# Down projections of a feed-forward stage as three fp32r products of upper and lower parts, in eight places

## What is computed

```
x = x + tanh(g_ffn[0]) * ffn(layernorm(x))

g = xf @ gate_w.T * gate_s            # [2048, 256] x [256, 704]
u = xf @ up_w.T * up_s
hdn = silu(g) * u                     # [2048, 704]
out = hdn @ down_w.T * down_s         # [2048, 704] x [704, 256]
```

## Time and profile before

| | before |
|---|---|
| time, median of 3 runs | 1323.59 us (1321.86 to 1324.62) |
| the profiled execution: time, span | 1321.55 us, 1319.8 us |
| TensorE (PE) busy | 1245.9 us, 94% of the span |
| VectorE (DVE) busy | 1084.2 us, 82% |
| ScalarE (ACT) busy | 966.9 us, 73% |
| GpSimd (POOL) busy | 701.7 us, 53% |
| chain that ended last, by engine | PE 78%, DVE 10%, issue 4%, ACT 3% |
| mean granted clock of TensorE | 0.986 |

### The profile page before, as it was taken

The page is one execution under the profiler, slowest core; times in us unless marked ns, Lnnn a source line. Parts: engine busy times, 40 slices in busy tenths (PEclk is TensorE's granted clock), DMA queues, the critical chain, the costliest instruction groups (busy, mean ns, idle before and its releaser), DMA issues.

```text
span 1319.8 us, 28439 instructions
## 1 busy us (share of the span) xinstructions
PE 1245.9 (94%) x10516; PEld 1086.0 (82%) x10516; DVE 1084.2 (82%) x2196; ACT 966.9 (73%) x2157; POOL 701.7 (53%) x612
## 2 busy tenths in 40 slices
PE   1678999999999999999999999999999999998998
PEld 1578899999999999999999999987776555555998
DVE  8979879999989999989999898986634778876654
ACT  5799888789987889898789897755322366674775
POOL 5666655656656557556556554433100255664685
PEclk9879999999999999999999999999999999998999
DMA  4212232231122322223321111222664413126762
GB/s 149 82 60 81 97 92 73 79 87 52 58 84 66 96 77 47 71 76 74 91 72 35 33 39 28 74 73 71 109 117 99 104 41 74 46 85 187 265 230 80
DMA packets 117511, 114.00 MB, mean 86 GB/s; under 512 B 12411, under 2 KB 102491, under 8 KB 116768
## 3 DMA queue, kind: packets, MB, share of 16 engines
q1 hardware_dynamic: 115152, 106.11, 28.9%
q0 software_dynamic: 2048, 6.05, 1.3%
q10 hardware_dynamic: 176, 0.04, 0.0%
HBM read 80.20 MB, written 32.00 MB: 85 GB/s over the span
## 4 chain that ended last, share of the span: by engine, by line
PE 78%; DVE 10%; issue 4%; ACT 3%; POOL 2%; DMA 2%; SPq 0%; POOLq 0%; ACTq 0%; DVEq 0%
PE PC L599 8%; PE PO L581 7%; PE SS L565 7%; PE B L542 5%; PE PA L498 4%; PE PA L500 4%; PE B L1293 3%; PE B L1784 2%; PE PA L512 2%; PE PA L511 2%; PE PA L510 2%; PE PC L589 2%; PE PO L1277 2%; PE B L555 2%; PE SS L568 2%
## 5 line engine op out<-in xcount | busy, mean ns | idle before, releaser
L1093 POOL TENSOR_TENSOR RB<-YS,M 128x512 bf16<-128x512 f32 x128 | 162.9, 1273 | 305.6 <-DVE YS L928 305.6
L718 ACT ACTIVATE QT<-B,sm 128x256 f32<-128x256 f32 x256 | 132.0, 572 | 42.0 <-PE B L542 41.9
L498 PE MATMUL PA<-WH,XQ 128*128 128x256 f32 x512 | 140.7, 306 | 17.2 <-DVE WL L874 13.3
L1088 POOL TENSOR_TENSOR yy<-vv,half 128x14 f32<-128x14 f32 (+1 forms) x64 | 147.9, 2311 | 5.3
L565 PE MATMUL SS<-QT,KT 128*128 128x256 f32 x512 | 131.8, 380 | 0.7 <-DVE mx L878 0.7
L500 PE MATMUL PA<-WL,XQ 128*128 128x256 f32 x512 | 130.1, 286 | 0.0
L898 DVE TENSOR_TENSOR QN<-QN,yy 128x512 f32<-128x512 f32 x128 | 127.5, 996 | 0.5 <-POOL yy L1088 0.5
L741 ACT ACTIVATE PPP<-SS 128x512 f32<-128x512 f32 x128 | 77.8, 608 | 65.8 <-PE SS L568 65.8
L890 DVE TENSOR_REDUCE vv<-SQ 128x7 f32<-128x896 f32 (+1 forms) x128 | 120.8, 944 | 0.3 <-ACT SQ L764 0.3
L498 PEld LDWEIGHTS PA<-WH,XQ 128*128 128x128 f32 x512 | 98.9, 193 | 18.8 <-DVE WL L874 13.7
L542 PE MATMUL B<-identf,QN 128*128 128x128 f32 x768 | 105.6, 274 | 2.0 <-ACT LNT L673 2.0
(11 more groups left out here) (354 smaller groups left out, 4109.3 us busy)
## 6 DMA issues: line engine op xcount, KB each, us to landing
W<-in_w SPq DMA_DIRECT2D x16, 1024.0 KB
XK<-xk_d SPq DMA_DIRECT2D x24, 512.0 KB, 4.3
V<-v_d SPq DMA_DIRECT2D x112, 64.0 KB
v_d<-VST SPq DMA_DIRECT2D x48, 128.0 KB, 2.1
Q<-qsc SPq DMA_DIRECT2D x8, 768.0 KB, 10.6
WR<-in_wprojT SPq DMA_DIRECT2D x16, 256.0 KB, 3.0
xk_d<-XK SPq DMA_DIRECT2D x8, 512.0 KB, 3.9
kt_d<-KT SPq DMA_DIRECT2D x64, 64.0 KB, 1.7
```

What stands on the lines that cost most here:

```text
L498: pe.matmul(PA[:, 256 * k:256 * k + 256], XQ[:, k, c, bs], wh[:, c, 256 * k:256 * k + 256], start=c == 0, stop=False)
L718: a.activation(QT[i % 2][:, o:o + 256], B1[:, o:o + 256], ACT.Identity, bias=col(n + "b"), scale=col(n + "w"))
L1088: p.tensor_tensor(yy[j % 2][:, :, 0:n], v_, half[:, 0:2 * n].rearrange("p (h k) -> p h k", h=2), ALU.pow).then_inc(s_rstd, 1)
L1093: p.tensor_tensor(RB[i % 2][:], YS[:], M[:], ALU.subtract).then_inc(s_rb, 1)
```

## The change

Hidden features and down weights are split into an fp32r upper part and the fp32r lower remainder, and a down projection is three products of parts per slice: 18 matmuls where there were six. `dve_hidden` now writes back into `SG`; ScalarE copies the upper part to `HS` or `HS2` (`act_hidden_upper`), VectorE subtracts it for the lower part (`dve_hidden_low`, semaphore `s_hl`). `HS` and `HS2` are eight places that slices take by turns (`i % 8`). `SG` is free again when the lower part is done. The down weights are scaled in quad 0, their upper part is made by ScalarE, their lower part by GpSimd.

The downs of a quad now follow slice 1 of the next quad, for three quads; the last four stand in `pe_attention_1`. Raw blocks 0 to 3 move into quad 3, query transposes and projections move by some slices, keys parts move later by up to a slice or two, masks move to quad 2, and the mask row is loaded into another place. Quad 0's queries are loaded back only behind the masks.

```diff
@@ -1176,19 +1176,32 @@
...
-        HD = [sb(f"HD{i}", [128, NI, 512]) for i in range(2)]
...
+        HS = sb("HS", [128, NI, 2, 512], FR)
...
+        HS2 = sb("HS2", [128, 2, 2, 512], FR)
+        DW = DWS[:, 0:NI * H].rearrange("p (n c) -> p n c", n=NI)
+        DS = DWS[:, NI * H:NI * H + H]
...
@@ -1197,14 +1210,16 @@
...
+        def hidden_part(i, z):
+            slot = i % 8
+            return HS[:, slot, z, :] if slot < NI else HS2[:, slot - NI, z, :]
...
@@ -1218,7 +1233,7 @@
...
-            return {(0, 4): 0, (0, 5): 1, (1, 0): 2, (1, 1): 3}.get((q4, n))
+            return {(0, 5): (0,), (1, 0): (1,), (1, 1): (2, 3)}.get((q4, n), ())
...
@@ -1240,12 +1255,14 @@
...
+                if q4 == 2:
+                    sp.wait_ge(s_up, NI)
+                    sp.dma_start(mrow, maskrow.broadcast_to([128, NT])).then_inc(s_row, 16)
...
@@ -1282,16 +1299,17 @@
...
-                pe.wait_ge(s_dw, 1)
+                pe.wait_ge(s_pl, G + 1)
                 pe.wait_ge(s_xf, 8)
             if j == 0:
-                pe.wait_ge(s_hd, NI * q4 + NI)
+                pe.wait_ge(s_hl, NI * q4 + NI)
             if b >= 2:
                 pe.wait_ge(s_fx, b - 1)
             for n in range(NI):
                 m = 128 if n < 5 else 64
-                t = pe.matmul(ps_[:, 0:H], HD[q4 % 2][0:m, n, 128 * j:128 * j + 128], DW[0:m, n, :], start=n == 0,
-                              stop=n == NI - 1)
+                for k, (z, w) in enumerate(((0, DWH), (0, DWL), (1, DWH))):
+                    t = pe.matmul(ps_[:, 0:H], hidden_part(NI * q4 + n, z)[0:m, 128 * j:128 * j + 128], w[0:m, n, :],
+                                  start=n == 0 and k == 0, stop=n == NI - 1 and k == 2)
             t.then_inc(s_down, 1)
...
@@ -1340,13 +1359,15 @@
...
-                    if q4 > 1 and n == 3:
-                        pe_query_turn(pe, q4 - 2)
-                    if q4 > 1 and n == 5:
+                    if q4 > 1 and n == 0:
                         pe_query_proj(pe, q4 - 2)
-                if q4 in (1, 2):
-                    for b in range(4 * q4 - 4, 4 * q4):
-                        pe_down(pe, b)
+                    if q4 and n == 1:
+                        for b in range(4 * q4 - 4, 4 * q4):
+                            pe_down(pe, b)
+                    if q4 in (1, 2) and n == 5:
+                        pe_query_turn(pe, q4 - 1)
+                    if q4 == 3 and n >= 2:
+                        pe_raw(pe, n - 2)
...
@@ -1370,9 +1391,23 @@
...
-                a.wait_ge(s_hd, i - 1)
+                a.wait_ge(s_hl, i - 1)
...
+        def act_hidden_upper(a, i):
+            m = 128 if i % NI < 5 else 64
+            a.wait_ge(s_hd, i + 1)
+            if i == NI:
+                a.wait_ge(s_pl, G + 1)
+            if i >= 8:
+                a.wait_ge(s_down, 4 * ((i - 8) // NI) + 4)
+            a.activation(hidden_part(i, 0)[0:m], SG[i % 2][0:m, :], ACT.Copy).then_inc(s_hi, 1)
+
+        def act_down_weights(a):
+            a.wait_ge(s_dw, 1)
+            a.activation(DWH[:, 0:5, :], DW[:, 0:5, :], ACT.Copy)
+            a.activation(DWH[0:64, 5, :], DW[0:64, 5, :], ACT.Copy).then_inc(s_ph, 1)
...
@@ -1416,14 +1450,20 @@
...
-                    if keys_parts_at(q4, n) is not None:
-                        act_keys_parts(a, keys_parts_at(q4, n))
+                    if q4 or n:
+                        act_hidden_upper(a, NI * q4 + n - 1)
+                    if q4 == 3 and n == 5:
+                        act_hidden_upper(a, NI * q4 + n)
+                    if q4 == 0 and n == 3:
+                        act_down_weights(a)
+                    for k in keys_parts_at(q4, n):
+                        act_keys_parts(a, k)
                     if q4 == 0 and n == 5:
                         act_last_turn(a)
-                    if q4 > 1 and n == 3:
-                        act_query_turn(a, q4 - 2)
-                    if q4 > 1 and n == 5:
+                    if q4 > 1 and n == 0:
                         act_query_proj(a, q4 - 2)
+                    if q4 in (1, 2) and n == 5:
+                        act_query_turn(a, q4 - 1)
...
@@ -1441,11 +1481,14 @@
...
-            v.scalar_tensor_tensor(out=HD[q4 % 2][0:m, n, :], in0=bank[i % 2][1][0:m, :],
+            v.scalar_tensor_tensor(out=SG[i % 2][0:m, :], in0=bank[i % 2][1][0:m, :],
                                    scalar=sm[0:m, AT["up_s"] + n:AT["up_s"] + n + 1], in1=SG[i % 2][0:m, :], op0=ALU.mult,
                                    op1=ALU.mult).then_inc(s_hd, 1)
+
+        def dve_hidden_low(v, i):
+            m = 128 if i % NI < 5 else 64
+            v.wait_ge(s_hi, i + 1)
+            v.tensor_tensor(hidden_part(i, 1)[0:m], SG[i % 2][0:m, :], hidden_part(i, 0)[0:m], ALU.subtract).then_inc(s_hl, 1)
...
@@ -1519,28 +1562,34 @@
...
-                    if keys_parts_at(q4, n) is not None:
-                        dve_keys_parts(v, keys_parts_at(q4, n))
-                    if q4 == 1 and n == 3:
-                        dve_down_weights(v)
-                    if q4 == 1 and n == 4:
-                        dve_mask_row(v)
-                    if q4 == 1 and n == 5:
-                        dve_masks(v)
+                    if q4 or n:
+                        dve_hidden_low(v, NI * q4 + n - 1)
+                    for k in keys_parts_at(q4, n):
+                        dve_keys_parts(v, k)
                     if q4 == 0 and n == 0:
                         dve_layer_root(v, 3)
                     if q4 == 0 and n == 1:
                         dve_layer_scale(v, 1, 3)
+                    if q4 == 0 and n == 3:
+                        dve_down_weights(v)
+                    if q4 and n == 1:
+                        for b in range(4 * q4 - 4, 4 * q4):
+                            dve_down(v, b)
+                        dve_layer_root(v, q4 - 1)
                     if q4 == 1 and n == 2:
                         dve_routing_constants(v)
-                    if q4 > 1 and n == 1:
-                        dve_layer_scale(v, 2, q4 - 2)
-                    if q4 > 1 and n == 5:
+                    if q4 and n == 3:
+                        dve_layer_scale(v, 2, q4 - 1)
+                    if q4 == 2 and n == 2:
+                        dve_mask_row(v)
+                    if q4 == 2 and n == 4:
+                        dve_masks(v)
+                    if q4 > 1 and n == 0:
                         dve_query_proj(v, q4 - 2)
-                if q4 in (1, 2):
-                    for b in range(4 * q4 - 4, 4 * q4):
-                        dve_down(v, b)
-                    dve_layer_root(v, q4 - 1)
+                    if q4 == 3 and n == 5:
+                        dve_hidden_low(v, NI * q4 + n)
+                    if q4 == 3 and n >= 2:
+                        dve_maximum_1(v, n - 2)
...
@@ -1564,6 +1613,9 @@
...
+            p.wait_ge(s_ph, G + 1)
+            p.tensor_tensor(DWL[:, 0:5, :], DW[:, 0:5, :], DWH[:, 0:5, :], ALU.subtract)
+            p.tensor_tensor(DWL[0:64, 5, :], DW[0:64, 5, :], DWH[0:64, 5, :], ALU.subtract).then_inc(s_pl, 1)
...
@@ -1696,7 +1748,9 @@
...
-                sp.wait_ge(s_hd, 12 * q4 + 12)
+                sp.wait_ge(s_up, 12 * q4 + 12)
+                if q4 == 0:
+                    sp.wait_ge(s_mask, 1)
...
@@ -1863,14 +1915,13 @@
...
-            for i in range(8):
+            pe_query_turn(pe, 2)
+            for i in range(4, 8):
                 pe_down(pe, 8 + i)
                 pe_raw(pe, i)
                 if i == 4:
                     pe_max_turn(pe, 0)
                 if i == 5:
-                    pe_query_turn(pe, 2)
-                if i == 6:
                     pe_query_proj(pe, 2)
...
```

More of the change, by code:

```diff
@@ L230, in build @@
         s_c, s_ch, s_ctx = (sem(n) for n in ("c", "ch", "ctx"))
-        s_sc, s_sr, s_srv = (sem(n) for n in ("sc", "sr", "srv"))
+        s_sc, s_sr = sem("sc"), sem("sr")
         s_rsm = [sem("rsm0"), sem("rsm1")]
@@ L1178, in build @@
         T16 = sb("T16", [128, 4096])
-        DW = sb("DW", [128, NI, H])
-        DS = sb("DS", [128, H])
-        HD = [sb(f"HD{i}", [128, NI, 512]) for i in range(2)]
-        GR = HD[0][:].rearrange("p n t -> p (n t)")[:, 0:4 * INTER].rearrange("p (w c n) -> p w c n", w=2, c=2)
+        DWH = sb("DWH", [128, NI, H], FR)
+        caus = sb("caus", [128, 128])
+        mcol = sb("mcol", [128, NB], I32)
+        fill4 = sb("fill4", [128, 112])
+        with nc.sbuf_tensor("GR", [128, 2, 2, INTER], F32) as GR:
+            pass
+        HS = sb("HS", [128, NI, 2, 512], FR)
+        with nc.sbuf_tensor("mrow", [128, NT], I32) as mrow:
+            pass
+        mrow = mrow[:]
+        mrf = mrow.bitcast(F32)
         XH, XL = [], []
@@ L1189, in build @@
         GL = sb("GL", [128, 2, 2, INTER], FR)
-        fill3 = sb("fill3", [128, 256])
         SG = [sb(f"SG{i}", [128, 512]) for i in range(2)]
+        DWL = sb("DWL", [128, NI, H], FR)
+        fill3 = sb("fill3", [128, 352])
```

(26 more changed lines are left out.)

25 lines of the change are left out of this document (8 added, 17 removed).

## The result

The changed kernel takes 1328.5 us (median; 1325.55 to 1333.69), the kernel before beside it on the same chip 1322.22 us (1320.43 to 1325.51). The ratio is **1.0048, 95% interval 1.0034 to 1.0062: 6.3 us slower**. The ratios of this document leave out one execution, of 3096.6 us, of the kernel e13. The forecast was "no change", with 1324.5; the time lies at the upper end of the range.

What follows compares the result with a forecast made beforehand. TensorE was taken as the bound. Saving 12.5 us and 0.3, against stops of 1.6, 1.6, 4.4, 4.4 and 1.0, gave +0.2 us, plus 0.8 for clock: 1322.5 profiled, 1324.5 forecast, range 1318 to 1328.5.

Steps and rivals of the forecast that it cites:

- 16 downs: TensorE's down projections: 18 fp32r products at 0.120 us, 2.16 us a block instead of 2.94, 12.5 us less in all.
- old idle time: TensorE's existing wait for a hidden slice around the end of quad 0 goes: 0.3 us less.
- stop 1: Slice 4: TensorE waits 1.6 us for gate product 6, as ScalarE's down-weight copies stand ahead of activation 4.
- stop 2: Slices 3 to 5: GpSimd holds VectorE's lower parts; TensorE waits 1.6 us, then 4.4 us before the first down.
- stop 3: Behind the second down: the third waits 4.4 us for VectorE's addition, queued behind keys parts and lower parts.
- small waits later: Three small TensorE waits in quad 3 and before the last four downs: 1.0 us more in all.
- low clock behind 937: Idle gaps of stops 2 and 3 may halve TensorE's clock; counted as 0.8 us more.
- old dip: Half clock near 1049 us in the kernel before, costing 1.5 us; the faster rival said it need not recur.
- Half its price: A clock dip of 1.5 us after stops 2 and 3 taken as about even odds, so 0.8 us counted.
- faster rival: Lower parts of slices 3 and 5 slip past GpSimd and no dip follows: 1320.1 us, tail to 1311; chance 0.28.
- slower one: TensorE's clock stays low past 948 us, longer than 5 us: 3.75 us more, 1327.5 us; chance 0.23.
- Late queries: Quad 0's queries, loaded behind the masks, arrive late for the first raw block: 1330 us or more; chance 0.03.

Runs made afterwards that it cites:

- e13: e12 with the load of quad 2's queries put back at its place in the changed kernel; ratio 0.9965 to the kernel before.
- e9: Changed kernel plus 15 useless products on TensorE ahead of its wait for the lower part of slice 5; ratio 1.0056 to the kernel before.
- e1: Changed kernel with the 64-row sixth slice padded to 128 rows with zero weights in every down projection; ratio 1.0022 to the kernel before.
- e5: Changed kernel with each down's three 64-row products placed singly between 128-row ones, six height changes a block instead of two; ratio 1.0183 to the kernel before.
- e2: Kernel before with the last slice padded to 128 rows, still six f32 products a block; ratio 0.9967 to the kernel before.
- e6: Changed kernel with GpSimd's lower part of quad 3's inputs held until the lower part of slice 5 is done; ratio 1.0053 to the kernel before.
- e4: Changed kernel with keys part 3 one slice later, behind slice 2 of quad 1; ratio 1.0040 to the kernel before.
- e14: e12 with the four keys parts moved behind slices 6, 8, 10 and 11; ratio 0.9937 to the kernel before, median 1314.98 us.
- e3: Changed kernel with quad 2's queries loaded behind the maxima of block 2 instead of block 1; ratio 1.0053 to the kernel before.
- e12: Changed kernel: padded slice, later quad 2 queries, later keys part 3, GpSimd's quad 3 lower part behind slice 5, down-weight scaling a slice earlier; ratio 0.9949 to before.
- e15: The changed kernel run once more, unedited; ratio 1.0046 to the kernel before, runs from 1324.64 to 1335.91 us.
- e10: Changed kernel with the four downs behind the third slice of the next quad instead of the second; ratio 1.0045 to the kernel before.

## Why the prediction was wrong

Right in kind: small against its parts, TensorE's saving given back in stops. Wrong in size by 5.5 us: the sum of the steps was +1.0 us, the traces show +6.6. By its own steps (the terms of the right column add up to +6.5):

| step | predicted | measured |
|---|---|---|
| 16 downs | -12.5 | -6.8 at full clock |
| old idle time | -0.3 | -0.3 |
| stop 1, gate 6 | +1.6 | +1.3 |
| stop 2, gate 7 and first down | +1.6, +4.4 | +0.8, +3.9 |
| stop 3, third down | +4.4 | +2.6, and 4.1 where the clock ahead is full (e9) |
| small waits later | +1.0 | +0.2 |
| low clock behind 937 | +0.8 | +1.6, taken off stop 3 |
| maxima row, its clock, old dip | 0 | +2.2 |
| rest of TensorE's work up to the first scores | 0 | +1.0 |

**What TensorE saves** is the step that failed: "nothing is cheaper than 0.120 there, and 0.13 (a switch between forms) would make it 9.6". The 0.120 was right for the product; the rows it came from have one height, and a down has two. (No row that the prediction names shows the 0.13 either.) e1 and e5 put the missing price at 0.19 us for each change of height. It stood in the trace of before: the 11.73 us of the earlier trace rows contain it as well (10.36 in e2), and the average of 0.244 a pass, 11.73 / 48, hid it. I divided a total by its count. TensorE's timeline of before puts the twelve passes of a block into one row and hides it too, but the timeline of its weight loads (PEld) shows two steps out of line, one on either side of the 64 rows:

```profile
945.41 0.29 PEld L1293 LDWEIGHTS B<-DW,HD 64*128 64x128 f32 x2 [0.33 <-issue]
946.03 0.94 PEld L1293 LDWEIGHTS B<-DW,HD 128*128 128x128 f32 x5 [0.33 <-issue]
```

The loads of this line sat idle for 8.7 us in 28 such places in the kernel before, and for 1.4 us in 6 once padded (e2).

The step is worth 5.7 us, as much as the whole error; 16 x 0.32 = 5.1 of it are the changes of height. The other errors cancel almost: the stops are 8.8 us and not 13.0, while the low clock costs 0.8 more than forecast, and the maxima row (2.2) and the rest of TensorE's work (1.0) were put at nothing.

**The stops** were found at the right instructions and with the right releasers, and the forecast made each somewhat too long; at gate product 7 that is because lower part 3 ended behind the first of GpSimd's two subtractions and not behind both. e6 confirms the hold by GpSimd (0.67 without, 1.62 with), and e4 and e14 the keys ahead of the additions. The prediction extended the hold to the lower parts from the Trainium skill's GPSIMD Engine Reference (1. Specifications), which says that GpSimd shares its SBUF interfaces with VectorE instructions of two SBUF inputs. The trace agrees: 2.20 and 1.62 us beside GpSimd, 0.67 alone.

**"Half its price" for a clock dip** was the wrong question. The dip came (0.61 and 0.82 in the windows of 3 us behind 937) and cost nothing in that trace, since stop 3 shrank by as much: e3, e9 and the changed kernel have the third down at one distance from the origin whatever the clock.

**The old dip at 1049** was named in the faster rival as a gain that might come. It did go in this trace (1.00 in 1048 to 1052), though not in e1's. What I did not ask is what had been hidden behind it. The maxima row was there to be priced: the load takes 10.3 us to landing, and the row is behind it in the same queue. e2 shows the pair most plainly: no dip, and 1.28 us of wait.

**The rivals.** The faster one had two of its conditions come true: lower part 3 slipped in between GpSimd's two subtractions, and the dip at 1049 did not recur. Together they were too small against the price of a down. The slower one had the size (1327.5) but not the mechanism: in the profiled execution the clock was back at 1.00 from 943.3 to 955. Low clock past 948 does occur: e6 and e5 ran at 0.50 until about 956 and 962. Low clock is the likely reason why the executions of the changed kernel spread over 8 us (those of e12 over 6), as the mean clocks of e15 suggest; the place of it is not shown. Late queries did not come in any trace of the changed kernel; the only wait for them is the 0.59 us of e14.

## What to carry to other kernels

Price a matmul from a stretch with the same sequence of shapes, and look inside one group before dividing a total by its count: a tail slice with fewer rows costs a change of height on the way in and out, and padding it with zeros gained 0.33% in the kernel before (e2) for a few changed lines. Before counting a vanished stall as gain, look for what it had been covering, on the DMA queue too. When a stop is set by another engine's queue, look at what stands ahead of the producer: here neither moving the consumer (e10) nor keeping TensorE at work (e9) helped, and moving the keys parts did (e14).

## What the runs showed of the hardware that I had not expected

- A change between weights of 128 and 64 rows cost 0.19 us each time, with fp32r (0.193 in e5) and with f32 ((11.73 - 10.36) / 7 = 0.196 inside a quad's downs, e2).
- A transfer that lands in 1.8 us took 8.0 when it was issued 6 us behind a load of 1.5 MB on the same queue; moving the load behind it removed TensorE's wait.
- Fifteen products without use held the granted clock at 1.00 through a wait (e9), and a wait of 4.1 us right behind was followed by 9 us at 0.50.
